# A weight preparation less in the first mixture, and a second layer whose transposes, derivative and projections are one block

## The chip, the cores and the metric

One core of a Trainium2 chip runs the whole network in one launch. Five engines work side by side, each from its own queue in program order, and wait for each other on semaphores: TensorE (PE in the profile; PEld is its weight load), VectorE (DVE), ScalarE (ACT), GpSimd (POOL) and SyncE (SP), which issues the transfers. The metric is the device time of the launch in microseconds, lower is better, as the median of several runs.

## The reference, cut to what matters

The network has two layers over 2048 tokens (2 sequences of 1024) of width 256. The first layer ends in a mixture of 16 experts, of which each token uses four. The second layer begins with a discrete reaction-diffusion derivative of the stream, then differential attention on it:

```python
lap_x = yp_x[:, :, :-2] - 2.0 * y + yp_x[:, :, 2:]      # along the features, reflected
lap_y = yp_y[:, :-2, :] - 2.0 * y + yp_y[:, 2:, :]      # along the tokens, reflected
du_dt = zX * lap_x + zY * lap_y + zR * y * (1.0 - y)
q, k, v = du_dt @ Wq.T, du_dt @ Wk.T, du_dt @ Wv.T      # q is scaled by 32 ** -0.5
```

Then come softmax attention, an output projection, a subject-wise linear layer and a second mixture with one expert for each token.

## The kernel before

**First mixture** (`experts_phase`, L1530 to L1715). TensorE works off jobs of 256 tokens, expert by expert. All engines run loops over pairs of experts in use; the number of pairs is read from a register at run time. While TensorE computes with one expert's weights, SP loads the next and GpSimd splits them into a rounded part and a rest (`split`, casts at L1607 and L1619, subtractions at L1613 and L1623) for single-pass products. `following(p, q)` gives pair `p` the splits 2p+1 and 2p+2, so the last turn loads and splits one set of weights more than TensorE uses. On the last expert `split` of that set runs beside the products. VectorE adds each job's result to the stream `X` at L1709.

**Between the layers** (L2723) all semaphores are cleared behind a barrier of all engines.

**Transposes** (`transpose_phase`, L431): a block of its own. TensorE turns `X` (tokens on partitions) into `hT` (features on partitions) by 32 transposes of 128x128, in 8 groups of 4 with a PSUM bank each; ScalarE and VectorE copy the groups out in turn (L453). A block ends when every engine has ended its part.

**Derivative and projections** (`laplace_phase`, L1718). The tokens are 4 windows of 512 (`w`), the features 2 halves of 128 (`f`); `bank(w, f)` is a PSUM bank for each pair. TensorE first multiplies `hT` by the second-difference operator `lap`, kept among the constants (L1765), 16 full fp32 products of 512 columns. GpSimd sums the two neighbours of each token into `nb` (L1809), then clears `qz`, the zero-padded queries (L1813). VectorE puts the derivative `du` together in four instructions for each (w, f): L1831 and L1832 for the reaction term, L1834 for the neighbours, L1836 for TensorE's part from PSUM. `du` lives in `att`. Then TensorE makes keys (L1750) and queries (L1758), 16 fp32 products each, and values (L1781), 32 of 256 columns. Keys and queries leave PSUM in two parts: ScalarE writes the rounded part (`kh` L1790, `qh` L1795), VectorE the rest (`kl` L1843, `ql` L1850). VectorE copies the values (L1868). GpSimd places the first three tiles of queries into `qz` (`place_queries`, L1879).

A full fp32 product stands in the profile as two MATMUL records. `product3` (L1521) is the cheaper form for operands split in two parts: three single-pass products, high by high, high by low, low by high.

**Attention** (`attention_phase`) is the next block, and needs queries, keys and values.

The diff touches these functions:

## Time and profile before

| what | us |
|---|---|
| median of 3 runs | 1523.15 |
| lowest and highest | 1522.03, 1525.4 |
| the profiled execution, its own time | 1524.83 |
| its span, first to last instruction | 1523.0 |
| last product of the first mixture | 978.0 |
| first transpose of the second layer | 985.4 |
| first instruction of the attention block | 1053.76 |

The profiled execution's time is its span and 1.8 us around it. Its stages are read by their place in the span: the first mixture runs until 978, the change of layers until 985, transposes until 992, derivative and projections until 1053.8, attention after that.

### The profile page before, as it was taken

What the parts mean: (1) busy time and instruction counts of PE and PEld (TensorE: products, weight loads), DVE (VectorE), ACT (ScalarE), POOL (GpSimd) and SP (SyncE); (2) the same over time, 40 slices, a digit from 0 to 9 for tenths busy, and PEclk for the clock granted to TensorE, in tenths of its full rate; (3) what the DMA queues carried; (4) which work ended last, traced back from release to release, by engine and by line L of the source; (5) the groups of instructions that cost most, each with busy time, mean ns of one, the idle gap of its engine ahead of it and who ended that gap; (6) DMA issues with size and microseconds to landing.
All of it is one profiled execution on the core that took longest, in us unless ns stands there. A gap on an engine that the chain in (4) does not pass through costs nothing. (4 is left out here: it accounts for less than half of the span.)

```text
span 1523.0 us, 24894 instructions
## 1 busy us (share of the span) xinstructions
PE 1372.9 (90%) x8678; PEld 1139.8 (75%) x8679; DVE 943.2 (62%) x1708; ACT 722.7 (47%) x1473; POOL 497.7 (33%) x478
## 2 busy tenths in 40 slices
PE   8866799978998789999999999888899899867998
PEld 3345356667895479999999999736688688647997
DVE  4955879965566854454343343395777777464776
ACT  3423877635122246555445556312555456333543
POOL 0331089830000234274062040442211210043885
PEclk9976989989998969999999999999999999988999
DMA  6000000010000014021011000050000000533550
GB/s 235 1 1 0 14 1 1 1 56 1 1 1 0 1 60 162 0 99 67 0 50 60 0 0 0 0 166 1 1 1 1 1 1 1 194 120 115 193 198 20
DMA packets 23244, 69.50 MB, mean 46 GB/s; under 512 B 4419, under 2 KB 8915, under 8 KB 18242
## 3 DMA queue, kind: packets, MB, share of 16 engines
q1 hardware_dynamic: 20866, 62.51, 11.8%
q0 software_dynamic: 2304, 6.03, 1.1%
q8 instruction: 43, 0.70, 0.2%
q14 instruction: 31, 0.25, 0.1%
HBM read 54.62 MB, written 14.19 MB: 45 GB/s over the span
## 5 line engine op out<-in xcount | busy, mean ns | idle before, releaser
L1702 DVE TENSOR_TENSOR ehidl<-hT,ehidh 128x512 fp32r<-128x512 f32 x148 | 140.4, 960 | 136.5 <-ACT ehidh L1685 135.9
L1679 ACT ACTIVATE hT<-ps,eb 128x256 f32<-128x256 f32 x296 | 124.4, 472 | 165.8 <-PE ps L1521 165.8
L2010 ACT ACTIVATE pr<-ps,nmax 128x256 f32<-128x256 f32 (+7 forms) x128 | 94.1, 739 | 103.4 <-DVE nmax L2040 103.3
L1521 PE MATMUL ps<-kh,qz 128*128 128x512 f32 (+3 forms) x384 | 125.3, 380 | 3.3 <-ACT pr L2010 1.9
L1709 DVE SCALAR_TENSOR_TENSOR X<-ps,wE,X 128x256 f32 x74 | 35.8, 484 | 108.3 <-PE ps L1521 98.7
L1685 ACT CAST ehidh<-hT 128x512 fp32r<-128x512 f32 x148 | 91.9, 621 | 4.7
L2040 DVE TENSOR_REDUCE nmax<-ps 128x1 f32<-128x256 f32 (+7 forms) x128 | 91.0, 748 | 1.2 <-PE ps L1950 0.6
L1603 POOL TENSOR_TENSOR eb<-eb1s,consts 128x8 f32<-128x8 f32 x8 | 2.1, 260 | 273.6 <-PE ps L1521 267.3
L1521 PEld LDWEIGHTS ps<-kh,qz 128*128 128x128 f32 x384 | 76.2, 199 | 13.3 <-ACT pr L2010 4.7
L1521 PE MATMUL ps<-ew_1h,ehidh 128*128 128x256 f32 x304 | 85.5, 281 | 0.5 <-POOL ew_1l L1623 0.5
L1521 PE MATMUL ps<-hTh,ew_1h 128*128 x304 | 85.4, 281 | 0.1
L1521 PE MATMUL ps<-ew_1l,ehidh 128*128 128x256 f32 x304 | 85.3, 281 | 0.0
L1521 PE MATMUL ps<-ew_1h,ehidl 128*128 128x256 f32 x304 | 85.3, 281 | 0.0
L1521 PE MATMUL ps<-hTh,ew_1l 128*128 x304 | 85.3, 281 | 0.0
L1521 PE MATMUL ps<-hTh,ew_0h 128*128 x288 | 82.2, 285 | 2.9 <-issue 2.9
L1521 PE MATMUL ps<-hTl,ew_1h 128*128 x304 | 84.7, 279 | 0.0
L1879 POOL CAST qz<-qh 32x256 fp32r<-32x256 f32 x64 | 27.5, 429 | 175.0 <-PE ps L1950 155.3
L1970 PE MATMUL ps<-v,hT 128*128 128x64 f32 x576 | 77.0, 279 | 5.1 <-ACT hT L2001 4.8
L1521 PE MATMUL ps<-hTh,ew_0l 128*128 x288 | 81.6, 283 | 0.0
L1521 PE MATMUL ps<-hTl,ew_0h 128*128 x288 | 81.3, 282 | 0.0
L1521 PE MATMUL ps<-ew_0h,ehidh 128*128 128x256 f32 x288 | 80.5, 280 | 0.0
L1521 PE MATMUL ps<-ew_0l,ehidh 128*128 128x256 f32 x288 | 80.4, 279 | 0.0
(524 smaller groups left out, 4303.1 us busy)
## 6 DMA issues: line engine op xcount, KB each, us to landing
ew1s<-in_ew_dram SPq DMA_DIRECT2D x9, 1024.0 KB, 4.7
ew2s<-in_ew_dram SPq DMA_DIRECT2D x9, 1024.0 KB, 6.8
fw1s<-in_fw_dram SPq DMA_DIRECT2D x8, 1024.0 KB, 7.6
fw2s<-in_fw_dram SPq DMA_DIRECT2D x8, 1024.0 KB, 9.4
slot_rows<-fill SPq DMA_DIRECT2D x1, 5140.0 KB, 20.1
xr<-slot_rows SPq DMA_DIRECT2D x8, 514.0 KB, 4.1
xT<-in_xT_dram SPq DMA_DIRECT2D x4, 512.0 KB, 7.6
X<-in_x_dram SPq DMA_DIRECT2D x1, 2048.0 KB, 18.2
```

The costliest lines, as they stand in the source:

```text
L1521: last = nc.tensor.matmul(out, lhs[a], rhs[b], start=(start and n == 0), stop=(stop and n == 2), **kw)
L1603: nc.gpsimd.tensor_tensor(b1[q][:, :], b1s[q][:, :], k.const("ones", 0, FB), ALU.mult)
L1679: nc.scalar.activation(hid[:, f, :], ps[:, f // 2, (f % 2) * JOB:(f % 2 + 1) * JOB], ACT.Gelu, bias=b1[q][:, f:f + 1]).then_inc(k.e_act, 1)
L1685: nc.scalar.copy(hidp[0][:, f - 1:f + 1, :], hid[:, f - 1:f + 1, :]).then_inc(k.e_dhi, 1)
L1702: nc.vector.tensor_tensor(lo[:, f, :], hid[:, f, :], hi[:, f, :], ALU.subtract).then_inc(k.e_lo, 1)
L1709: nc.vector.scalar_tensor_tensor(x, ps[:, DOWN + t, 0:E], wE2[:, bass.ds(e * NT + blk * TILES + t, 1)], x, ALU.mult, ALU.add).then_inc(k.e ...
L1879: last = nc.gpsimd.tensor_copy(k.qz[r, i % QZ, n, :, s, :], part[r, :, i * P:(i + 1) * P])
L1970: last = nc.tensor.matmul(ps[:, PV + i % 2, h * 64:(h + 1) * 64], dT[:, n % 2, j, :], k.v[:, i - c + j, h * 64:(h + 1) * 64], start=(h == ...
L2010: nc.scalar.activation(pr[:, n % 3, u, 0:wide], half(n, u, wide), ACT.Exp, bias=nmax[:, n % 2, u:u + 1], accum_out=sums[:, u, n:n + 1]).th ...
L2040: nc.vector.tensor_reduce(nmax[:, n % 2, u:u + 1], half(n, u, wide), AX.X, ALU.max, negate=True).then_inc(k.a_max, 1)
```

## The change

In the mixture the pairs of loads and splits are turned by one: load 1 and split 1 come ahead of the loop, and the loop runs one time less (at least once), so the set of weights that no job uses is neither loaded nor split.

In the second layer the transposes lose their block and join `laplace_phase`. The stream, the derivative and the weights are split in two parts and multiplied as single-pass products: two for each step of the second-difference operator (which is rounded only), three for keys, queries and values. ScalarE does all copies of the transposes, the rounded parts, the first half of the reaction term and the copies of the values; VectorE the low parts and the neighbours, which it adds straight from `hT`; GpSimd clears `qz` in six pieces and no longer sums neighbours. The values no longer come last but between the keys and queries of their bank. The order in each queue is written out by hand. The weights are loaded with `wk` first.

```diff
-            return (p * 2 + 1, 1, p + 1) if q == 0 else (p * 2 + 2, 0, p + 2)
+            return p * 2 + (q + 2), q, p + 2
+
+        def later_pairs(eng, name):
+            rest = eng.alloc_register(f"{name}_later_pairs")
+            eng.reg_alu(rest, entry(eng, "pairs", 0, E0 // 2), -1, ALU.add)
+            eng.reg_alu(rest, rest, 1, ALU.max)
+            return eng.snap(rest, min_val=1, max_val=E0 // 2 - 1)
...
-            pairs = entry(sp, "pairs", 0, E0 // 2)
+            rest = later_pairs(sp, "sp")
+
+            def load(s, parity):
+                sp.wait_ge(k.e_s2, s + 1)
+                load_first_mixture(sp, k, entry(sp, "sel", s, E0 - 1), parity)
+
             sp.wait_ge(k.r_b2, NT // 2)
-            with sp.Fori(0, pairs) as p:
+            load(1, 1)
+            with sp.Fori(0, rest) as p:
                 for q in range(2):
                     s, parity, loads = following(p, q)
-
-                    sp.wait_ge(k.e_s2, s + 1)
-                    load_first_mixture(sp, k, entry(sp, "sel", s, E0 - 1), parity)
+                    load(s, parity)
 
         @block.gpsimd
...
-            pairs = entry(pool, "pairs", 0, E0 // 2)
+            rest = later_pairs(pool, "pool")
             for g in range(NT // 2):
                 nc.gpsimd.tensor_tensor(k.X[:, 2 * g:2 * g + 2, 0:E], k.X[:, 2 * g:2 * g + 2, 0:E],
                                         k.bo[g // 4][:, 2 * g % 8:2 * g % 8 + 2, :], ALU.add).then_inc(k.r_b2, 1)
             pool.wait_ge(k.e_s1, 1)
             pool.wait_ge(k.e_s2, 3)
-            with pool.Fori(0, pairs) as p:
+            split(1, 1, 1)
+            with pool.Fori(0, rest) as p:
                 for q in range(2):
...
+            def turn(w, f):
+                for j in range(4):
+                    last = nc.tensor.transpose(ps[:, bank(w, f), j * P:(j + 1) * P],
+                                               k.X[:, 4 * w + j, f * P:(f + 1) * P], k.const("ident"))
+                last.then_inc(k.t_5, 1)
+
+            def second_difference(w, f):
+                pe.wait_ge(k.l_lap, 1)
+                pe.wait_ge(k.l_yl, EB * (w + 1))
+                for j in range(EB):
+                    for n in range(2):
+                        last = nc.tensor.matmul(ps[:, bank(w, f), :], lap[:, j * E + f * P:j * E + (f + 1) * P],
+                                                parts[n][:, j, window(w)], start=(j == 0 and n == 0),
+                                                stop=(j == EB - 1 and n == 1))
+                last.then_inc(k.l_mm, 1)
+
+            def weighted(w, f, weight, done):
+                for j in range(EB):
+                    last = product3(nc, ps[:, bank(w, f), :], [x[:, j, f * P:(f + 1) * P] for x in weight],
+                                    [x[:, j, window(w)] for x in parts], j == 0, j == EB - 1)
+                last.then_inc(done, 1)
+
+            def keys(w, f):
+                pe.wait_ge(k.l_wl, SPLIT.index(KEY) + 1)
+                pe.wait_ge(k.l_dl, EB * (w + 1))
+                weighted(w, f, wk, k.l_km)
+
+            def queries(w, f):
+                pe.wait_ge(k.l_wl, SPLIT.index(QUERY) + 1)
+                pe.wait_ge(k.l_v, EB * w + f + 1)
+                weighted(w, f, wq, k.l_qm)
+
+            def values(w, f):
+                pe.wait_ge(k.l_wl, SPLIT.index(VALUE) + 1)
+                pe.wait_ge(k.l_kl, EB * w + f + 1)
+                for t in range(2):
+                    i = 4 * w + 2 * f + t
                     for j in range(EB):
-                        last = nc.tensor.matmul(ps[:, bank(w, f), :], k.wk[:, j, f * P:(f + 1) * P],
-                                                du[:, j, w * W:(w + 1) * W], start=(j == 0), stop=(j == EB - 1))
-                    last.then_inc(k.l_km, 1)
-
-            def queries(w):
-                for f in range(EB):
-                    pe.wait_ge(k.l_kl, EB * w + f + 1)
-                    for j in range(EB):
-                        last = nc.tensor.matmul(ps[:, bank(w, f), :], k.wq[:, j, f * P:(f + 1) * P],
-                                                du[:, j, w * W:(w + 1) * W], start=(j == 0), stop=(j == EB - 1))
-                    last.then_inc(k.l_qm, 1)
-
-            for w in range(NW):
-                for f in range(EB):
-                    for j in range(EB):
-                        last = nc.tensor.matmul(ps[:, bank(w, f), :],
-                                                k.const("lap", j * E + f * P, P), k.hT[:, j, w * W:(w + 1) * W],
-                                                start=(j == 0), stop=(j == EB - 1))
-                    last.then_inc(k.l_mm, 1)
-            pe.wait_ge(k.s_wC, 64)
-            keys(0)
-            for w in range(1, NW):
-                keys(w)
-                queries(w - 1)
-            queries(NW - 1)
-            for i in range(NT):
-                if i < 8:
-                    pe.wait_ge(k.l_ql, i + 1)
-                else:
-                    pe.wait_ge(k.l_v, i - 7)
-                for j in range(EB):
-                    last = nc.tensor.matmul(ps[:, i % 8, 0:E], du[:, j, i * P:(i + 1) * P], k.wv[:, j, :],
-                                            start=(j == 0), stop=(j == EB - 1))
+                        last = product3(nc, ps[:, bank(w, f), t * E:(t + 1) * E],
+                                        [x[:, j, i * P:(i + 1) * P] for x in parts], [x[:, j, :] for x in wv],
+                                        t == 0 and j == 0, j == EB - 1, skip_group_check=True)
                 last.then_inc(k.l_vm, 1)
+
+            turn(0, 0)
+            turn(0, 1)
+            turn(1, 0)
+            turn(1, 1)
+            second_difference(0, 0)
+            second_difference(0, 1)
+            turn(2, 0)
+            turn(2, 1)
+            second_difference(1, 0)
+            keys(0, 0)
+            keys(0, 1)
+            values(0, 0)
+            turn(3, 0)
+            turn(3, 1)
+            second_difference(1, 1)
+            second_difference(2, 0)
+            values(0, 1)
...
+            def growth(w):
+                b = w // 2
+                act.wait_ge(k.l_z, 1)
+                act.wait_ge(k.l_ya, EB * (w + 1))
+                nc.scalar.activation(du[:, :, window(w)], k.hT[:, :, window(w)], ACT.Identity, bias=z[:, 1, b:b + 1],
+                                     scale=z[:, 0, b:b + 1]).then_inc(k.l_a, 1)
+
+            def high_weight(n):
+                act.wait_ge(k.s_wC, 16 * 4)
+                nc.scalar.copy(PARTS[n][0][:, :, :], WHOLE[n][:, :, :]).then_inc(k.l_wh, 1)
+
+            def operator():
+                nc.scalar.copy(lap[:, :], k.const("lap", 0, EB * E)).then_inc(k.l_lap, 1)
+
+            def high_derivative(w, f):
+                act.wait_ge(k.l_mm, EB * (w + 1))
+                act.wait_ge(k.l_du, EB * w + f + 1)
+                nc.scalar.copy(k.qh[:, f, window(w)], du[:, f, window(w)]).then_inc(k.l_dh, 1)
+
+            def high_keys(w, f):
+                act.wait_ge(k.l_km, EB * w + f + 1)
+                nc.scalar.copy(k.kh[:, f, window(w)], ps[:, bank(w, f), :]).then_inc(k.l_k, 1)
+
+            def values(w, f):
+                act.wait_ge(k.l_vm, EB * w + f + 1)
+                i = 4 * w + 2 * f
+                nc.scalar.copy(k.v[:, i:i + 2, :], ps[:, bank(w, f), :].rearrange("p (t e) -> p t e", t=2)
+                               ).then_inc(k.l_v, 1)
+
+            def high_queries(w, f):
+                act.wait_ge(k.l_qm, EB * (w + 1))
+                nc.scalar.activation(k.qh[:, f, window(w)], ps[:, bank(w, f), :], ACT.Copy,
+                                     scale=SCALE).then_inc(k.l_q, 1)
+
+            high_weight(0)
+            stream(0, 0)
+            high(0, 0)
+            stream(0, 1)
+            growth(0)
+            stream(1, 0)
+            high(0, 1)
+            stream(1, 1)
+            operator()
+            growth(1)
+            high_weight(2)
+            high(1, 0)
+            high(1, 1)
+            high_weight(1)
+            stream(2, 0)
+            high_derivative(0, 0)
+            stream(2, 1)
+            high(2, 0)
...
+            def clear(q):
+                for part in range(2):
+                    nc.gpsimd.memset(k.qz[:, q, part, :, :, :].bitcast(F32), 0.0).then_inc(k.l_zero, 1)
+
+            clear(0)
             nc.gpsimd.memset(k.fill[:, 0:ROWF - 1], 0.0).then_inc(k.z_fill, 1)
             nc.gpsimd.memset(k.fill[:, ID].bitcast(I32), OUTSIDE).then_inc(k.z_fill, 1)
+            pool.wait_ge(k.l_dl, EB * NW)
+            for q in range(1, QZ):
+                clear(q)
             pool.wait_ge(k.z_fill, 2)
-            pool.wait_ge(k.l_zero, 1)
+            pool.wait_ge(k.l_zero, 2 * QZ)
             pool.wait_ge(k.l_ql, EB)
...
+            def neighbours(w):
+                b, first = w // 2, w * W
+
+                def add(at, of, n):
+                    o = du[:, :, first + at:first + at + n]
+                    then(nc.vector.scalar_tensor_tensor(o, k.hT[:, :, first + of:first + of + n], k.row("zy", b), o,
+                                                        ALU.mult, ALU.add))
+
+                dve.wait_ge(k.l_ya, EB * (w + 2 - w % 2))
+                if w % 2 == 0:
+                    add(1, 0, W - 1)
+                    add(0, 1, 1)
+                    add(0, 1, W)
+                else:
+                    add(0, -1, W)
+                    add(0, 1, W - 1)
+                    add(W - 1, W - 2, 1)
+
+            def differences(w, f):
...
+            coefficients()
+            low_weight(0)
+            low(0, 0)
+            growth(0)
+            low(0, 1)
+            neighbours(0)
+            differences(0, 0)
+            differences(0, 1)
+            low(1, 0)
+            growth(1)
+            low(1, 1)
+            low_weight(2)
+            low_derivative(0, 0)
+            low_derivative(0, 1)
+            neighbours(1)
+            low_keys(0, 0)
...
-                transpose_phase(nc, k, k.X, k.hT, None, None, {"mm": k.t_5})
```

The order of all four queues goes on in the same manner to the last window. On TensorE it ends `queries(1, 1)`, `keys(3, 0)`, `keys(3, 1)`, `queries(2, 0)`, `values(2, 1)`, `values(3, 0)`, `queries(2, 1)`, `values(3, 1)`, `queries(3, 0)`, `queries(3, 1)`. On ScalarE `high_queries(0, 1)` stands behind `high_keys(3, 1)`. On VectorE `low_queries(0, 1)` stands right behind `low_derivative(3, 1)`.

## Rows read from the trace of the kernel before

**Rows 1.** The page: busy time of each engine.

```profile
PE 1372.9 (90%) x8678; PEld 1139.8 (75%) x8679; DVE 943.2 (62%) x1708; ACT 722.7 (47%) x1473; POOL 497.7 (33%) x478
```

**Rows 2.** Windows around the change: busy us (instructions) by engine, clock, DMA share.

```profile
978.00:985.30 7.30, 0.00 (x0) 0.00 (x0) 0.64 (x2) 0.00 (x0) 5.50 (x6) 0.78 0.00 0
...
991.70:1008.00 16.30, 13.97 (x32) 6.00 (x32) 15.89 (x11) 0.00 (x0) 13.58 (x9) 1.00 0.26 95
1008.00:1039.00 31.00, 29.74 (x64) 12.59 (x65) 25.72 (x39) 8.87 (x15) 11.18 (x24) 0.94 0.54 154
1039.00:1053.70 14.70, 14.01 (x65) 11.97 (x63) 7.38 (x17) 0.60 (x1) 0.00 (x0) 1.00 0.00 1
```

**Rows 3.** Timeline of GpSimd at the end of the mixture.

```profile
978.66 4.92 POOL L1623 TENSOR_TENSOR ew_0l<-ew2s,ew_0h 128x512 fp32r<-128x512 f32 x4
```

**Rows 4.** Timeline of VectorE, same stretch: the last addition to the stream.

```profile
978.41 0.48 DVE L1709 SCALAR_TENSOR_TENSOR X<-ps,wE,X 128x256 f32 x1 [0.26 <-DVE X L1709]
```

**Rows 5.** Timeline of TensorE: the transposes.

```profile
985.38 5.41 PE L443 MATMUL ps<-consts,X 128*128 128x128 f32 x32 [7.40 <-PEq L2723]
```

**Rows 6.** Windows through the transposes and at attention's start; clock third from last.

```profile
985.30:988.90 3.60, 3.52 (x17) 3.56 (x18) 0.69 (x1) 1.17 (x2) 0.00 (x0) 0.50 0.02 5
988.90:991.00 2.10, 1.89 (x17) 1.65 (x15) 1.56 (x3) 1.17 (x2) 0.00 (x0) 0.99 0.00 0
1053.70:1057.20 3.50, 1.86 (x16) 1.73 (x16) 1.85 (x10) 2.29 (x6) 0.00 (x0) 1.00 0.01 2
1057.20:1060.60 3.40, 2.91 (x16) 2.91 (x17) 1.96 (x10) 1.81 (x10) 0.00 (x0) 0.50 0.00 0
```

**Rows 7.** Timeline of ScalarE: first instruction of the attention block.

```profile
1053.76 1.28 ACT L1994 ACT_TABLE_LOAD   x1 [13.92 <-PEq L1722]
```

**Rows 8.** Groups by line and shape, 960 to 1060 us: busy us, mean ns.

```profile
L1750 PE MATMUL ps<-att,wk 128*128 128x512 f32 x32 | 16.4, 659 | 3.5 <-DVE att L1836 3.4
...
L1831 DVE TENSOR_SCALAR att<-hT,zc 128x512 f32<-128x512 f32 x8 | 11.2, 1397 | 0.0
...
L1834 DVE SCALAR_TENSOR_TENSOR att<-nb,rows,att 128x512 f32<-128x512 f32 x8 | 6.0, 756 | 0.3
...
L1843 DVE TENSOR_TENSOR kl<-ps,kh 128x512 fp32r<-128x512 f32 x8 | 5.3, 684 | 1.4 <-ACT kh L1790 1.3
L1813 POOL MEMSET qz<- 128x6144 f32 x1 | 5.2, 5214 | 0.0
...
L1790 ACT CAST kh<-ps 128x512 fp32r<-128x512 f32 x8 | 4.7, 586 | 30.4 <-PE ps L1750 30.4
```

**Rows 9.** Timeline of TensorE: single-pass products of 256 columns.

```profile
950.24 0.28 PE L1521 MATMUL ps<-ew_0h,ehidl 128*128 128x256 f32 x1
...
950.35 0.28 PE L1521 MATMUL ps<-ew_0h,ehidh 128*128 128x256 f32 x1
```

**Rows 10.** Timeline of TensorE: single-pass products of 512 columns.

```profile
1254.49 0.39 PE L1521 MATMUL ps<-kl,qz 128*128 128x512 f32 x1
1254.71 0.57 PE L1521 MATMUL ps<-kh,qz 128*128 128x512 f32 x2
```

**Rows 11.** Groups by shape on ScalarE, whole span: forms that the change adds.

```profile
L1685 ACT CAST ehidh<-hT 128x512 fp32r<-128x512 f32 x148 | 91.9, 621 | 4.7
...
L244 ACT ACTIVATE modT<-modT,bw 128x1024 f32<-128x1024 f32 x4 | 4.6, 1146 | 3.1 <-DVE modT L334 2.9
```

**Rows 12.** Groups by shape on VectorE, whole span: two inputs, 1024 elements.

```profile
L1250 DVE SCALAR_TENSOR_TENSOR negm<-both_m,fh,negm 128x1024 f32<-128x1024 f32 x1 | 1.3, 1285 | 0.0
```

**Rows 13.** Timeline of SyncE: the issue of the last weight.

```profile
993.11 0.43 SPq L1739 DMA_DIRECT2D wo<-in_wo_dram  x1
```

**Rows 14.** Transfers issued from 985 to 1030 us: KB each, us to landing.

```profile
wo<-in_wo_dram SPq DMA_DIRECT2D x1, 256.0 KB, 4.4
```

**Rows 15.** Timeline of GpSimd: four casts of queries, beside two kinds of VectorE work.

```profile
1022.88 2.59 POOL L1879 CAST qz<-qh 32x256 fp32r<-32x256 f32 x4 [17.50 <-DVE ql L1850]
...
1028.11 1.71 POOL L1879 CAST qz<-qh 32x256 fp32r<-32x256 f32 x4
```

More of the change, by code:

```diff
@@ new lines, in _ @@
+            second_difference(2, 1)
+            keys(1, 0)
+            keys(1, 1)
+            queries(0, 1)
+            second_difference(3, 0)
+            second_difference(3, 1)
+            values(1, 0)
+            keys(2, 0)
+            keys(2, 1)
+            queries(1, 0)
+            values(1, 1)
+            values(2, 0)
+            queries(1, 1)
+            keys(3, 0)
+            keys(3, 1)
+            queries(2, 0)
+            values(2, 1)
+            values(3, 0)
+            queries(2, 1)
@@ L1798, in _, with stream, high @@
-            keys(0)
-            for w in range(1, NW):
-                keys(w)
-                queries(w - 1)
-            queries(NW - 1)
+            def stream(w, f):
+                act.wait_ge(k.t_5, EB * w + f + 1)
+                nc.scalar.copy(k.hT[:, f, window(w)], ps[:, bank(w, f), :]).then_inc(k.l_ya, 1)
+            def high(w, f):
+                act.wait_ge(k.l_ya, EB * w + f + 1)
+                nc.scalar.copy(k.qh[:, f, window(w)], k.hT[:, f, window(w)]).then_inc(k.l_yh, 1)
@@ new lines, in _ @@
+            coefficients()
[14 more added lines that the diff above has]
+            low_keys(0, 0)
+            differences(1, 0)
+            low_weight(1)
+            low(2, 0)
@@ new lines, in _ @@
+            low_keys(0, 1)
+            low(2, 1)
+            growth(2)
+            differences(1, 1)
+            low(3, 0)
+            low(3, 1)
+            low_derivative(1, 0)
+            low_derivative(1, 1)
+            neighbours(2)
+            low_keys(1, 0)
+            differences(2, 0)
+            growth(3)
+            differences(2, 1)
+            low_derivative(2, 0)
+            low_derivative(2, 1)
+            low_keys(1, 1)
+            neighbours(3)
+            differences(3, 0)
```

165 lines of the change are left out of this document (102 added, 63 removed).

## The prediction

> **What bounds the kernel now.** I read the page first: TensorE is busy for 90% of the span [rows 1], so a change counts where TensorE stands idle or where its own work shrinks. Then I cut the change's neighbourhood into windows [rows 2]. From 978.0 to 985.3 TensorE does nothing at all, while GpSimd works for 5.5 us. The timelines say with what: GpSimd's last four subtractions start at 978.66 and end at 983.58 [rows 3], on weights that no job uses, while VectorE's last addition to the stream ends at 978.89 [rows 4]. The transposes start at 985.38 [rows 5], 1.8 us behind GpSimd. So the change of layers waits for GpSimd.
>
> In the second layer the windows show TensorE busy 13.97 of 16.3 us, 29.74 of 31.0 and 14.01 of 14.7, with VectorE beside it at 15.89, 25.72 and 7.38 [rows 2]. First VectorE sets the pace, then both, then TensorE alone with the values. The transposes ran at a granted clock of 0.50 until 988.9 and at 0.99 after it, which are 1.2 and 2.4 GHz [rows 6]. Attention's first instruction is at 1053.76 [rows 7]. From the transposes' block, whose start I put 0.05 us ahead of its first product at 985.33, to there are 68.4 us. That is the stage to be rebuilt.
>
> **Part 1, the mixture.** The last turn's load and split go. The load has been over for long and costs nothing: no transfer runs in 978.0:985.3 [rows 2]. The split ends at 983.58; without it the barrier waits for VectorE at 978.89. I keep the 1.8 us from the last engine's end to the first transpose. Gain: 983.58 - 978.89 = 4.7 us. Bounds: nothing, if something else holds the barrier up; and 5.5 us, GpSimd's whole work in that window. The new order of loads ahead of the loop makes the same loads and splits in the same order, and TensorE's waits there are unchanged: nothing.
>
> **Part 2, work for each engine in the new block.**
> *TensorE.* A full fp32 product of 512 columns takes two records; the window with the second-difference products holds 32 records in 13.97 us, 0.87 us a product, and keys, queries and values are of the same size [rows 2, 8]. So before: 16 + 16 + 16 products and 14.0 us of values, 56 us. A single-pass product of 256 columns starts 0.11 us after the one before [rows 9], one of 512 columns 0.22 us [rows 10]. Now: second difference 32 x 0.22 = 7.1, keys and queries 96 x 0.22 = 21.3, values 96 x 0.11 = 10.6: 39 us. The 32 transposes are the same, 0.11 us each at the full clock (17 records in 1.89 us [rows 6]). TensorE loses 17 us of work, but not 17 us of time, since others now set the pace.
> *ScalarE.* A rounding copy from SBUF of 512 elements costs 0.62 us and one of 1024 with scale and bias 1.15 us [rows 11]; a copy from PSUM 0.59 us [rows 8]. Its queue: 20 copies from SBUF (3 weights, 1 operator, 8 stream, 8 derivative), 4 of 1024, 32 from PSUM: 12.4 + 4.6 + 18.9 = 36 us.
> *VectorE.* From 512 elements 0.68 us without a third operand, 0.76 with one [rows 8]; over 1024 elements with two inputs from SBUF 1.29 us [rows 12]. The neighbours of a window are two such instructions, one on two elements (0.2 us, an estimate: the 0.48 us that L1709 takes for 256 elements [rows 4], less 0.27, half of the step from 512 to 1024 elements) and three waits for the engine's own result: 2.85 us. Its queue: 35 of 0.69, 8 of 0.76, 4 of 1.29, 4 of 2.85: 46.8 us, of which consecutive independent instructions overlap by some 0.08 us each. The 11.2 us of L1831 (1.40 us each, stretched beside GpSimd) and the 6.8 us of value copies are gone, 19 low parts have come.
> *GpSimd.* Clearing qz took 5.21 us [rows 8]; each sixth 0.87. The neighbour sums go.
>
> **Part 3, the four queues laid side by side,** from the block's start T. An instruction starts when its engine is free and its last wait has fallen; from a product's last column to a reader in PSUM I allow 0.2 us, to TensorE from another engine 0.15.
> - ScalarE's queue begins with `high_weight(0)`, which waits for all four weights. The fourth is issued at 993.11, 1.34 us after its block's start [rows 13], and lands 4.4 us later [rows 14]: T + 5.75. Behind it stand all copies of the transposes, so the block as a whole starts there; the four groups of transposes are long done. This is the change's own new wait. Lower bound 4.4, if the issues were no hindrance.
> - ScalarE then needs ten instructions to the end of `operator`: T + 11.4. VectorE's `low(0, 1)` ends at 11.3. TensorE starts the second difference at 11.5, at the low clock after 9.6 us of idling: until 15.1.
> - VectorE: neighbours(0) until 14.1, both differences until 16.0, then low(1, 0), growth(1), low(1, 1), low_weight(2), low_derivative(0, 0) and (0, 1): T + 20.4. Only now may TensorE make keys(0, 0), at 20.5.
> - From neighbours(1) to low_derivative(3, 1) VectorE has 29 steps (3 neighbours, 2 growths, 6 differences, 18 others) of 27.9 us; 2.0 overlap and 0.8 of short waits come in: it ends at T + 47.0. TensorE in that stretch has 25 us of work (10 x 1.33, 5 x 1.32, 5 x 0.89 and two groups of transposes) and short waits.
> - keys(3, 0) follows at 47.4. From there nine products and groups of values stand without a gap: 6 x 1.33 + 3 x 1.32 and two short waits, until 59.6; then ScalarE's two copies and VectorE's last low queries: 61.75.
> - GpSimd may clear four sixths from 47.0, until 50.5, and place queries once low_queries(0, 1) has ended, at 52.1. That is 24 casts in fours of 1.71 us [rows 15], 10.3 us: T + 62.4. It is last, by 0.7 us.
>
> With the full clock throughout, the same working ends at 61.7; with the low clock lasting a few microseconds longer into the keys, at 64.2. I take 63.0 in the middle, and 0.3 us to attention's first instruction (the old block's last value copy ends at 1053.47). So 63.3 against 68.4: gain 5.1 us.
>
> The Trainium skill (TensorE: Matmul & The Clock Gate, Part 4: PE-mode transpose) says that transposes don't bring the full clock. By it the transposes of windows 2 and 3, 16 of them, would cost 0.1 us more each, 1.7 us. The trace speaks against it: through 17 transposes and nothing else the clock was 0.50 and it then rose to 0.99 [rows 6].
>
> **Sum.** 4.7 + 5.1 = 9.8 us off the profiled execution's 1524.83 gives 1515.0; that execution lies 1.7 us above the median of the runs, so the median becomes 1513.3.
>
> **The rivals.**
> *The placing of queries sets the end, at its slow rate.* Four casts took 2.59 us at 1022.88, where VectorE ran two-input additions from SBUF, and 1.71 at 1028.11, where one input came from PSUM [rows 15]. In the new tail VectorE's low keys and queries read one input from PSUM, so I hold it for less likely. At 2.59 the block ends at T + 67.6: 5.2 us more, 1518.5.
> *The clock: slower.* At 1053.70:1057.20 TensorE was busy 1.86 of 3.5 us, and the clock stood at 0.50 for the window after it [rows 6]. If the breaks in the new queue keep it at 0.50 through the keys as well, the last nine products alone cost 12.0 us more, 1525.3; with half of the 25 us in the middle at half speed too, 24.5 us more, 1538. It decides from 9.8 us lost, that is, 9.8 us of TensorE's work at the low clock on the path. Against it: from 20.5 on TensorE has work for over 90% of the time, and the window 1008.00:1039.00 kept 0.94 with a break in it [rows 2].
> *The mixture gives nothing:* the barrier waits for something other than GpSimd. 4.7 us more, 1518.0. GpSimd's end and the transposes' start, 1.8 us apart, speak against it.
> *The start is quicker:* weights at T + 4.4 and the full clock end the block at 60.3, 2.7 us less: 1510.6.
>
> **How the numbers follow.** Forecast 0.60 (own range 1510 to 1517: 61.7 to 64.2 for the clock, and VectorE 5% off either way, 2 us); slow placing 0.12; clock 0.08; nothing from the mixture 0.06; quicker start 0.14. The range takes in the slow placing, the mixture's failure with some of the clock, and below the quick start with 5.5 us from the mixture and VectorE 5% faster: 1507.5 to 1520. A change under 0.2%, 3 us, can't be told from none here. Faster: all but the clock and the chance that two of the dearer cases meet, 0.91. Slower 0.05, the heavy form of the clock; same 0.04, its lighter form or two mishaps.
>
> **What would show it.** The transposes start near 980.7. ScalarE's first instruction of the block is the copy of `wk`, some 5.8 us after that. TensorE idles from about T + 2 to T + 11. VectorE is busy nearly without a break from T + 20 to T + 47. Attention starts near 1044. GpSimd's last cast and VectorE's last low queries end within 1 or 2 us of each other. The prediction is wrong if the weights land later than T + 7, if the clock is below 0.9 from T + 20, if VectorE's instructions over two halves cost well over 1.3 us, or if a wait written by hand stands crosswise so that TensorE idles in its last nine pieces.

## The result, and the profile after

| kernel | median, us | lowest to highest | runs | ratio to before, 95% |
|---|---|---|---|---|
| before | 1522.81 | 1522.03 to 1525.4 | 9 | |
| after | 1516.37 | 1513.87 to 1520.71 | 9 | 0.9957 [0.9947, 0.9968] |

The change makes the kernel faster by 6.4 us; 9.8 were forecast, and 1516.37 against the 1513.3 predicted lies inside the range. The profiled execution after took 1516.37 us, with a span of 1514.6. The page, busy time of each engine [rows 1]:

```profile
PE 1361.2 (90%) x8742; PEld 1147.2 (76%) x8743; DVE 934.0 (62%) x1699; ACT 742.6 (49%) x1509; POOL 470.9 (31%) x459
```

TensorE's busy time is 11.7 us less than before, VectorE's 9.2 and GpSimd's 26.8; ScalarE's is 19.9 more. Windows around the change, with busy us and instructions by engine, clock, DMA share and GB/s [rows 2, 6]:

```profile
976.70:978.40 1.70, 0.00 (x0) 0.01 (x1) 0.00 (x0) 0.00 (x0) 0.03 (x1) 1.00 0.00 0
978.40:984.50 6.10, 1.94 (x16) 1.71 (x16) 1.08 (x2) 0.00 (x0) 2.35 (x4) 0.99 0.79 264
984.50:999.00 14.50, 6.46 (x20) 4.60 (x20) 11.73 (x16) 11.79 (x20) 0.00 (x0) 0.62 1.06 295
999.00:1021.00 22.00, 21.67 (x111) 18.41 (x112) 20.67 (x28) 10.66 (x18) 0.00 (x0) 0.94 0.07 20
1021.00:1040.00 19.00, 19.00 (x111) 16.18 (x109) 9.60 (x16) 8.94 (x17) 10.72 (x23) 1.00 0.00 1
1040.00:1042.90 2.90, 0.09 (x1) 0.00 (x0) 1.29 (x2) 1.09 (x3) 2.36 (x6) 0.92 0.00 0
```

In the first stretch TensorE does nothing; its whole break between the layers is 2.65 us, by the timeline below, where it was 7.40. Then comes a stretch of 6.1 us with 1.94 us of transposes and the transfers at 264 GB/s: the new wait for the weights. From 984.5 VectorE and ScalarE work at 11.7 of 14.5 us each. In 999:1021 VectorE has 20.67 of 22.0, but TensorE has 21.67, and from 1021 TensorE is busy without a break and VectorE half the time. The last 2.9 us are the copies and casts behind the last product.

The timeline of the same stretch, with the last addition to the stream first [rows 3 to 5, 7, 15]:

```profile
976.17 0.48 DVE L1720 SCALAR_TENSOR_TENSOR X<-ps,wE,X 128x256 f32 x1 [0.26 <-DVE X L1720]
```

```profile
978.41 1.94 PE L1766 MATMUL ps<-consts,X 128*128 128x128 f32 x16 [2.65 <-PEq L2936]
990.20 0.76 PE L1775 MATMUL ps<-qh,lapr 128*128 128x512 f32 x1 [9.85 <-ACT lapr L1870]
990.76 0.63 PE L1775 MATMUL ps<-ql,lapr 128*128 128x512 f32 x1
```

```profile
984.50 0.62 ACT L1867 CAST wk_h<-wk 128x512 fp32r<-128x512 f32 x1 [12.86 <-DMA wo<-in_wo_dram]
...
1042.89 1.28 ACT L2207 ACT_TABLE_LOAD   x1 [1.68 <-PEq L1731]
```

```profile
1026.17 3.63 POOL L1953 MEMSET qz<- 128x1024 f32 x4 [45.42 <-DVE ql L2017]
1032.09 1.70 POOL L2092 CAST qz<-qh 32x256 fp32r<-32x256 f32 x4 [2.30 <-DVE ql L2027]
...
1040.88 1.70 POOL L2092 CAST qz<-ql 32x256 fp32r<-32x256 f32 x4
```

The last addition ends at 976.65 and the transposes start at 978.41, 1.8 us behind it. With the block's start T at 978.36, as in the prediction 0.05 ahead of the first transpose, ScalarE begins at T + 6.1, released by the transfer of `wo`; the second difference begins at T + 11.8, and its products stand 0.42 to 0.56 us apart, at the low clock. GpSimd's last casts end at T + 64.2 and attention starts at T + 64.5.

From these rows the way from before to after can be added up by stage, in profiled spans (1523.0 to 1514.6, 8.4 us). Attention is taken from its first instruction to the start of its last product of scores:

| stage | before | after | gain |
|---|---|---|---|
| all ahead of the last addition to the stream, its start | 978.41 | 976.17 | 2.2 |
| from there to T | 6.92 | 2.19 | 4.7 |
| T to attention's first instruction | 68.4 | 64.5 | 3.9 |
| attention, to its last product of scores | 237.6 | 239.3 | -1.7 |
| the rest | | | -0.7 |

The first line can't be put down to the change. In fourteen profiles of kernels with and without it that addition starts between 975.4 and 979.4: at 978.4, 977.5 and 975.4 with the old mixture, at 975.5 to 979.4 with the new. Without it the gain of this pair would be 6.2 us, which is what the medians say. The fourth line was nobody's forecast and needed experiments.

### The profile page after: what moved, and what is told of

Same layout as the page of the kernel before. It is cut to its first block and busy times, and to the rows that moved or that the text cites. A ratio compares the mean times of both kernels' runs of the same rounds, so it can differ in the third digit from the quotient of the medians.

```text
span 1514.6 us, 25020 instructions
## 1 busy us (share of the span) xinstructions
PE 1361.2 (90%) x8742; PEld 1147.2 (76%) x8743; DVE 934.0 (62%) x1699; ACT 742.6 (49%) x1509; POOL 470.9 (31%) x459
## 5 line engine op out<-in xcount | busy, mean ns | idle before, releaser
L1521 PE MATMUL ps<-kh,qz 128*128 128x512 f32 (+3 forms) x384 | 128.5, 388 | 5.5 <-DVE maskb L2237 3.3
L1521 PEld LDWEIGHTS ps<-kh,qz 128*128 128x128 f32 x384 | 78.9, 206 | 15.5 <-ACT pr L2223 4.7
L1521 PE MATMUL ps<-ew_0h,ehidl 128*128 128x256 f32 x288 | 80.6, 280 | 0.0
L2183 PEld LDWEIGHTS ps<-v,hT 128*128 128x128 f32 x576 | 71.4, 196 | 7.5 <-ACT hT L2214 4.7
```

What stands on the lines that cost most here:

```text
L1521: last = nc.tensor.matmul(out, lhs[a], rhs[b], start=(start and n == 0), stop=(stop and n == 2), **kw)
L2183: last = nc.tensor.matmul(ps[:, PV + i % 2, h * 64:(h + 1) * 64], dT[:, n % 2, j, :], k.v[:, i - c + j, h * 64:(h + 1) * 64], start=(h == ...
```

## The experiments

All kernels of an experiment ran beside the kernel before. "Block" is T to attention, "attention" as in the table above, both from the one profiled execution.

| kernel | median, us | ratio to before, 95% | block | attention |
|---|---|---|---|---|
| before | | | 68.4 | 237.6 |
| null_before | 1524.11 | 0.9995 [0.9985, 1.0005] | 69.2 | 237.3 |
| mix_alone | 1519.47 | 0.9957 [0.9944, 0.9970] | 68.2 | 237.4 |
| layer_alone | 1520.95 | 0.9981 [0.9969, 0.9994] | 63.8 | 238.9 |
| after_again | 1516.85 | 0.9950 [0.9933, 0.9966] | 63.9 | 239.0 |
| warm_tail | 1516.84 | 0.9947 [0.9933, 0.9961] | 65.8 | 238.8 |
| warm_head | 1514.46 | 0.9932 [0.9917, 0.9946] | 64.3 | 237.6 |
| start_early | 1512.10 | 0.9910 [0.9893, 0.9927] | 60.5 | 237.6 |
| early_queries | 1514.93 | 0.9937 [0.9922, 0.9953] | 63.7 | 237.6 |
| both_edits | 1512.89 | 0.9932 [0.9919, 0.9945] | 58.9 | 240.4 |
| full_products | 1523.79 | 0.9997 [0.9986, 1.0007] | 70.2 | 237.8 |
| neighbours_pool | 1522.74 | 0.9986 [0.9975, 0.9998] | 69.1 | 239.0 |
| late_attention | 1519.58, one run | | 65.9 | 240.5 |

### The two parts alone

`null_before` is the kernel before under another name, `after_again` the changed kernel, `mix_alone` the change of the mixture with the old second layer, `layer_alone` the reverse: `following(p, q)` and the loops as before, with the new `laplace_phase`.

> The kernel before against itself, profiled a second time. Both theories: a ratio of 1.000 within 0.2%. It is run for its trace. If the change's profile owes its 1.0 us between the mixture's first addition and the second expert, and its 1.8 us more in attention, to chance (the place at which the clock falls), the same stages of this trace lie up to 2 us beside those of the first trace of before. If they are effects of the change, this trace repeats before's within 0.3 us: 68.1 us and 237.6 us.

> The changed kernel once more, for a second trace. Ratio 0.9957 as on record. If attention's 1.8 us more are an effect of the change, its stage again takes 239 us; if chance, it lies anywhere from 237 to 240. The block from first transpose to attention: 64.5 us again by my theory, within 1 us by where the clock rises.

> The mixture's part alone: the unused load and split are gone, the second layer is as before. My theory: the transposes start 1.8 us behind VectorE's last addition and not 6.5 us, 4.7 us less, ratio 0.9969; the block behind it takes its old 68.4 us. Rival, the barrier waits for something else: ratio 1.000. Rival, the turned loop also speeds the mixture's start by the 1.0 us seen in the profile after: 5.7 us less, ratio 0.9963, and the stage from the first addition to the second expert's first product takes 67.1 us and not 68.1.

> The second layer's part alone: the mixture keeps its unused load and split. My theory: the block from first transpose to attention takes 64 to 65 us and not 68.4, attention as before, so 3.9 us less, ratio 0.9974. Rival, attention really takes 1.8 us more behind the new block (its 237.6 us become 239.3, because the clock is worse there): 2.1 us less in all, ratio 0.9986, and attention's stage again near 239.

The same kernel twice comes out at 0.9995, with an interval down to 0.9985. `null_before` also shows how far the block moves by itself: 69.2 us, where the first profile of the same kernel had 68.4. The microsecond between the mixture's first addition and the second expert's first product, of which two expectations speak, is chance: the stage takes 68.0 us in both profiles of before and in `mix_alone`, but 67.0 in `layer_alone`, which has the old mixture, and 67.1 and 67.9 in the two profiles of the changed kernel.

In `mix_alone` the last addition to the stream, on VectorE, and the first transposes, on TensorE:

```profile
979.28 0.48 DVE L1720 SCALAR_TENSOR_TENSOR X<-ps,wE,X 128x256 f32 x1 [0.26 <-DVE X L1720]
```

```profile
981.52 3.84 PE L443 MATMUL ps<-consts,X 128*128 128x128 f32 x21 [2.65 <-PEq L2734]
```

The addition ends at 979.76 and the transposes start at 981.52: 1.8 us again. The stretch from the addition's start to T is 2.2 us, where it was 6.9; the block behind it, 68.2, and attention, 237.4, are those of before. So the mixture is worth 4.7 us, as forecast, in this and in the ten other profiles with it (2.2 us against 6.9 in all of them). The ratio, 0.9957, says 6.6 us with 4.6 at the edge of its interval, which agrees. `layer_alone` has a block of 63.8, 4.6 us shorter, and gives 2.9 us by its ratio: attention takes 1.5 back. By their ratios the two parts add up to 9.5 us, the whole gives 6.5 and 7.6; each interval is 1 to 2 us wide to either side, so these runs do not tell the sum from the whole.

### The wait for the weights

In `start_early` the copy of the first weight no longer stands at the head of ScalarE's and VectorE's queues, but behind `operator` and behind `low(1, 1)`:

```diff
-            high_weight(0)
             stream(0, 0)
...
             operator()
+            high_weight(0)
...
-            low_weight(0)
             low(0, 0)
...
             low(1, 1)
+            low_weight(0)
```

> The changed kernel with the first weight's high part moved behind the operator on ScalarE, and its low part beside the second weight's on VectorE; the stream's copies then don't wait for the weights. My theory: the wait for the weights, 6.1 us from the block's start, sets the block's start, and the block takes 4 to 4.5 us less: 60 us; ratio against before 0.993. Rival, the pace of the keys sets the block and the start only fills a wait: under 1 us less.

The timeline of ScalarE, and of TensorE:

```profile
980.64 0.59 ACT L1852 COPY hT<-ps 128x512 f32<-128x512 f32 x1 [7.43 <-PE ps L1766]
...
985.07 0.63 ACT L1870 CAST lapr<-consts 128x512 fp32r<-128x512 f32 x1
985.59 0.62 ACT L1867 CAST wk_h<-wk 128x512 fp32r<-128x512 f32 x1
```

```profile
979.98 2.81 PE L1766 MATMUL ps<-consts,X 128*128 128x128 f32 x16 [2.64 <-PEq L2936]
985.83 0.76 PE L1775 MATMUL ps<-qh,lapr 128*128 128x512 f32 x1 [3.05 <-ACT lapr L1870]
```

With T at 979.93, ScalarE starts at T + 0.7 on the first transposes and the second difference at T + 5.9, not 11.8. The copy of `wk` comes at 985.59, T + 5.7, about as soon as it did behind its wait, and the first keys wait for VectorE's low part of the derivative, not for it. The block is 60.5 us, 3.5 to 4.1 less than in the two profiles of the changed kernel, and the time 1512.10, with an interval below that of the change. Of the 5.9 us that the start gains some 2 are lost again on the way: the last low part of the derivative ends at T + 43.7 against T + 47.1 and 47.7, and from there the tail is as long as before. The loss goes with the granted clock. A window from T + 14.6 to T + 21.4, clock third from last:

```profile
994.53:1001.36 6.83, 5.97 (x16) 4.84 (x17) 5.76 (x9) 1.07 (x2) 0.00 (x0) 0.50 0.96 284
```

The first keys start at T + 15.5 and run at half the clock for 5.9 us; in the two profiles of the changed kernel they did so for 1.8 and 2.3 us.

### The tail of queries

In `early_queries` ScalarE's `high_queries(0, 1)` moves from behind `high_keys(3, 1)` to right behind `high_queries(0, 0)`. `both_edits` is that and `start_early` together.

```diff
+            high_queries(0, 1)
...
-            high_queries(0, 1)
```

> The changed kernel with the high part of the queries (0, 1) made right behind that of (0, 0) on ScalarE, so that GpSimd can place queries some 2 us sooner. My theory: GpSimd ends last by 0.5 us in the profile after, VectorE's low queries right ahead of it; the block takes 0.3 to 0.6 us less and then ends with VectorE. Rival, the placing alone sets the end: 2 us less.

> The changed kernel with both earlier edits: the first weight's parts behind the operator, and the queries (0, 1) behind (0, 0) on ScalarE. My theory: the gains add, the block takes 59.7 to 60.0 us (60.5 less the 0.5 us by which GpSimd ended behind VectorE); ratio against before 0.990 to 0.991. Rival: with the front shortened another wait sets the end and it stays at 60.5.

The ends of the two queues in `early_queries`, GpSimd's and VectorE's, with T at 980.15:

```profile
1031.45 1.70 POOL L2092 CAST qz<-qh 32x256 fp32r<-32x256 f32 x4
...
1040.23 1.71 POOL L2092 CAST qz<-ql 32x256 fp32r<-32x256 f32 x4
```

```profile
1042.30 1.29 DVE L2027 SCALAR_TENSOR_TENSOR ql<-ps,qh 128x512 fp32r<-128x512 f32 x2 [2.57 <-ACT qh L1889]
```

The casts begin as soon as the clearing of `qz` is over and end at T + 61.8; now VectorE is last, at T + 63.4, and attention starts at T + 63.7 where it started at 63.9 and 64.5. In the changed kernel GpSimd was last by 0.5 us, and half a microsecond is what the edit gives: from the end of TensorE's last product to attention are 2.2 us, where they were 2.8 in both profiles of the changed kernel. In `both_edits` the block is 58.9, better by a microsecond than expected, and 5.0 to 5.6 less than in the changed kernel. That microsecond is the clock's: the first keys start at T + 15.5 again, but the low clock ended 2.9 us sooner than in `start_early`, and the last nine pieces began at T + 43.7, not 44.8.

```profile
994.33:997.75 3.42, 3.02 (x7) 2.47 (x8) 2.96 (x4) 0.09 (x1) 0.00 (x0) 0.50 0.99 290
997.80:1001.00 3.20, 3.12 (x21) 2.59 (x20) 2.65 (x5) 2.18 (x3) 0.00 (x0) 1.00 0.99 278
```

But attention takes 240.4 in its profile, and its ratio, 0.9932, missed the 0.990 to 0.991 expected. Both it and `start_early` are faster than before and than the change: the interval of `start_early` lies below both of the changed kernel's, that of `both_edits` below one of them.

### What each part of the new block carries

`full_products` makes keys, queries and values as full fp32 products from the whole derivative and the whole weights. The parts of the derivative and of the weights are still made, but no product reads them.

```diff
-                    last = product3(nc, ps[:, bank(w, f), :], [x[:, j, f * P:(f + 1) * P] for x in weight],
-                                    [x[:, j, window(w)] for x in parts], j == 0, j == EB - 1)
+                    last = nc.tensor.matmul(ps[:, bank(w, f), :], weight[:, j, f * P:(f + 1) * P],
+                                            du[:, j, window(w)], start=(j == 0), stop=(j == EB - 1))
...
```

> The changed kernel with keys, queries and values as full fp32 products of whole weights and whole derivative; everything else, the low parts too, is still made, only not used there. TensorE's work grows by 0.34 us for each of 16 groups of keys and queries and 0.27 for each of 8 groups of values, 7.6 us. My theory now: from 40 us on TensorE is the pace, and before that VectorE: the block takes 5 to 7 us more than 64 to 64.5, so the single-pass products carry more than the block's whole gain. Rival, VectorE is the pace nearly to the end: at most 3 us more.

Groups by line on TensorE, 978 to 1050 us:

```profile
L1782 PE MATMUL ps<-att,wk 128*128 128x512 f32 x32 | 15.6, 634 | 0.4 <-DVE ql L2017 0.4
L1782 PE MATMUL ps<-att,wq 128*128 128x512 f32 x32 | 14.9, 592 | 0.0
L1802 PE MATMUL ps<-wv,att 128*128 128x256 f32 x64 | 14.9, 380 | 0.0
```

TensorE's busy time in the block, T to attention, in `full_products` and in the changed kernel (first number behind the length):

```profile
978.79:1049.03 70.24, 56.67 (x192) 35.62 (x192) 45.83 (x61) 32.53 (x57) 15.41 (x32) 0.90 0.30 90
```

```profile
978.37:1042.90 64.53, 49.16 (x256) 40.91 (x256) 44.37 (x61) 32.48 (x57) 15.46 (x32) 0.89 0.34 98
```

That is 7.5 us more, as expected. The block is 70.2, 5.7 to 6.3 longer than in the changed kernel and longer than the three of before, 68.2 to 69.2: the cheaper products carry more than the block's whole gain.

`neighbours_pool` lets GpSimd sum the neighbours as before, and VectorE adds the sum in one instruction for each window; GpSimd's first clearing of `qz` moves behind those of `fill`:

```diff
+                nc.gpsimd.tensor_tensor(s[:, :, 1:T - 1], y[:, :, 0:T - 2], y[:, :, 2:T], ALU.add).then_inc(k.l_nb, 1)
...
-                dve.wait_ge(k.l_ya, EB * (w + 2 - w % 2))
-                if w % 2 == 0:
-                    add(1, 0, W - 1)
-                    add(0, 1, 1)
-                    add(0, 1, W)
...
+                dve.wait_ge(k.l_nb, 3 * (b + 1))
+                o = du[:, :, window(w)]
+                then(nc.vector.scalar_tensor_tensor(o, nb[:, :, window(w)], k.row("zy", b), o, ALU.mult, ALU.add))
```

> The changed kernel with the neighbours summed on GpSimd for each sequence, as before, and one addition per window on VectorE: 1.5 us less VectorE work in each of four windows. My theory: VectorE first waits for GpSimd (two sums of 3.6 us and more beside its own additions from SBUF), and TensorE is the pace behind, so nothing is won: block within 1 us of 64.2, or up to 3 us more. Rival, VectorE's load sets the block: 4 to 6 us less.

The timelines of GpSimd and VectorE:

```profile
993.20 3.88 POOL L1963 TENSOR_TENSOR nb<-hT 128x2044 f32<-128x2044 f32 x1 [9.23 <-ACT hT L1853]
997.04 0.34 POOL L1965 TENSOR_TENSOR nb<-hT 128x2 f32<-128x2 f32 x2
1012.62 3.89 POOL L1963 TENSOR_TENSOR nb<-hT 128x2044 f32<-128x2044 f32 x1 [15.24 <-ACT hT L1853]
```

```profile
997.42 1.28 DVE L2005 SCALAR_TENSOR_TENSOR att<-nb,rows,att 128x1024 f32<-128x1024 f32 x1 [3.79 <-POOL nb L1965]
...
1014.10 3.57 DVE L1987 TENSOR_TENSOR ql<-hT,qh 128x512 fp32r<-128x512 f32 x2 [0.25 <-ACT qh L1857]
1017.59 1.28 DVE L2015 TENSOR_TENSOR ql<-att,qh 128x512 fp32r<-128x512 f32 x2
```

It was expected within 1 us of the change to 3 us slower; it is 4.5 to 5.1 us in the block. VectorE waits 3.79 us for the first sum, though its own instruction is then 1.6 us shorter than the three that it replaces. The second sum runs beside VectorE's low parts of the stream: two of them take 3.57 us, 2.96 of it the first, where a pair of the same size takes 1.28 at 1017.59. A third part stands in a window; the clock is third from last:

```profile
1001.20:1007.90 6.70, 5.15 (x12) 3.87 (x13) 4.37 (x6) 1.44 (x3) 0.00 (x0) 0.57 0.39 107
```

TensorE's clock was 0.57 over these 6.7 us, through a second difference and the first keys; in the changed kernel it was back at the full clock 2.3 us into the keys. The clock's part need not be this edit's: `warm_tail`, below, has the same longer stretch at the low clock and a block 1.3 to 1.9 us longer. What is left is by this estimate some 3 us, so taking the sums off GpSimd was most likely a gain of its own.

### The clock at the start

TensorE idles ahead of the second difference, which then runs at the low clock. `warm_head` puts seven full fp32 products of constants into that gap, into a bank not in use:

```diff
+            idle_products(7, 7)
             second_difference(0, 0)
```

> The changed kernel with seven such products behind the first four groups of transposes, in the 10 us in which TensorE waits for the operator. My theory: the second differences then run at the full clock, 0.23 us a product and not 0.43, and the first keys too; the block takes 1.5 to 2 us less than 64.0 to 64.5. Rival, VectorE alone sets the pace there: the products are faster and the block ends no sooner than 64.0.

```profile
993.21 0.47 PE L1775 MATMUL ps<-qh,lapr 128*128 128x512 f32 x1 [2.50 <-ACT lapr L1875]
993.52 0.39 PE L1775 MATMUL ps<-ql,lapr 128*128 128x512 f32 x1
993.75 0.39 PE L1775 MATMUL ps<-qh,lapr 128*128 128x512 f32 x1
```

```profile
983.50:990.00 6.50, 6.50 (x21) 3.52 (x20) 1.39 (x2) 2.37 (x5) 0.21 (x2) 0.94 1.01 339
...
1001.50:1004.40 2.90, 2.71 (x7) 2.16 (x8) 2.75 (x4) 0.00 (x0) 0.00 (x0) 0.50 0.43 124
```

The clock is at 0.94 over the window with the added products, and the second difference starts with products 0.23 us apart. Its eighth ends at T + 14.5, 0.7 to 1.1 us sooner. But the keys run at 0.50 all the same, and low_derivative(0, 1) ends at T + 20.2 as in the changed kernel (20.2 and 20.6): VectorE sets the pace there. The block gains nothing, 64.3. The rival held.

### Attention's 1.5 us

Attention is unchanged and takes 237.3 to 237.8 us in seven profiles, 238.8 to 240.5 in the other seven. A window in the changed kernel, 167 us into attention, and the same place in the kernel before; clock third from last:

```profile
1209.80:1213.20 3.40, 3.40 (x15) 2.99 (x14) 1.96 (x4) 1.36 (x4) 0.37 (x1) 0.52 0.00 0
```

```profile
1220.30:1223.60 3.30, 3.30 (x26) 3.04 (x26) 2.60 (x5) 1.77 (x6) 0.44 (x2) 1.00 0.00 0
```

TensorE is busy throughout in both, with 15 products at a clock of 0.52 in the one and 26 at 1.00 in the other: 11 products less, at 0.13 us each 1.4 us. Each of the seven longer profiles has this stretch at the low clock, 3.4 us long; it begins 165.7 to 167.9 us behind attention's start, and none of the shorter seven has it. Just ahead of it TensorE has three short breaks, of 0.12, 0.27 and 0.76 us, and the clock falls within 0.5 us of the third one's end; but the shorter seven have the same three breaks, and it does not fall there. Two of the seven, `both_edits` and `late_attention`, have a further one at 45 us and take 240.4 and 240.5.

The first theory was that TensorE's idling ahead of attention brings it. `warm_tail` fills that gap with three full fp32 products behind the last queries, with results that nothing uses.

```diff
             queries(3, 1)
+            pe.wait_ge(k.l_ql, 1)
+            idle_products(3, 0)
```

> The changed kernel with three full fp32 products (512 columns, of constants, result unused) behind the last queries, into a bank already read; some 2.6 us in which TensorE otherwise waits for the block's end. My theory: attention's 239.0 to 239.3 us in the three traces with the new block, against 237.4 to 237.6 in the three with the old one, come from TensorE idling some 3 us ahead of attention, so that the clock is low for 10 to 14 us at its start. Then the stage returns to 237.5 us and the low stretch to 7 us, 1.6 us less in all, ratio against before 0.994. Rival, attention is slower for another reason (layout, queues): the stage stays at 239 us.

The theory fell. Attention's first 5.3 us were at the full clock (3.4 in the kernel before, none in the changed one), but the stretch is there, and attention took 238.8:

```profile
1209.80:1213.20 3.40, 3.40 (x16) 2.93 (x14) 1.96 (x4) 1.29 (x4) 0.40 (x1) 0.59 0.00 0
```

Nor does the low clock at attention's start cost anything that shows: in `early_queries` it lasts for attention's first 10 us, and attention takes 237.6. The block of `warm_tail` is longer, 65.8, because its first keys ran at half the clock for 5.9 us and not for 2.3: the low clock lasted 6.8 us there, as in `neighbours_pool` and `start_early`.

The second was that the clock's steps stand at fixed places and attention's start moves among them. `late_attention` delays attention with five such products in place of three.

> The changed kernel with five unused full products behind the last queries: the block ends 0.5 to 1.5 us later than in warm_tail's order of 64.2. All four traces with attention at 238.7 us or more have a stretch of low clock some 166.5 us behind attention's first instruction, none of the six at 237.4 to 237.6 has one. My theory: it is where the clock's steps fall relative to attention, and no effect of the change: the moved start gives 237.5 and no such stretch, more likely than not. Rival: the new block brings it in any case: 239 again.

It took 240.5, where 237.5 was held for more likely. The fourteen traces still speak for this theory. Each has another stretch at the low clock, which begins 128.8 to 131.6 us behind attention's start and so shows where the clock's steps stood. Sorted by it, the profiles with and without the later stretch fall into groups:

| that stretch begins, us behind attention's start | the later stretch |
|---|---|
| 128.8, 128.9, 129.0, 129.2 | in all four |
| 129.3, 129.5, 129.7, 129.7 | in none |
| 130.2, 130.4 | in both, and the one at 45 us |
| 130.8, 130.9 | in neither |
| 131.6, 131.6 | in one of two |

This order was found afterwards, and no experiment placed the steps on purpose. So the stretch, and its price, are shown; what decides that it comes is not. It is no property of the new block: `start_early`, `early_queries`, `warm_head` and `full_products` have new blocks and attention at 237.6 to 237.8.

## Why the prediction was right, and where it was short

- **The mixture: right.** 4.7 us forecast, 4.7 measured in eleven profiles with it against three without, with the 1.8 us of the barrier kept.
- **The wait for the weights: right.** T + 5.75 forecast, 5.1 to 6.5 in the nine profiles with the wait; `start_early` shows that it is a wait on the path, and worth 3.5 to 4.1 us. It is the largest thing that the change left lying.
- **VectorE sets the pace to T + 47: right to T + 20.** In the three profiles of the unedited block (the two of the changed kernel and `layer_alone`) low_derivative(0, 1) ended at T + 20.2 to 20.6 (20.4 forecast), and low_derivative(3, 1) at T + 47.0 to 47.7 (47.0). Its three instructions over two halves cost what was forecast, 2.85 us. But keys(3, 0), which the forecast started right behind the second, started 1.1 us after it: TensorE came to them late. `growth` was forecast at 1.15 us on ScalarE and takes 1.25, and on TensorE's side 0.22 and 0.11 us for a product were 0.23 and 0.12:

```profile
1024.38 0.28 PE L1521 MATMUL ps<-wv_h,qh 128*128 128x256 f32 x1
1024.50 0.29 PE L1521 MATMUL ps<-wv_l,qh 128*128 128x256 f32 x1
...
1027.20 0.39 PE L1521 MATMUL ps<-qh,wk_h 128*128 128x512 f32 x1
1027.43 0.39 PE L1521 MATMUL ps<-ql,wk_h 128*128 128x512 f32 x1
```

```profile
L1996 DVE SCALAR_TENSOR_TENSOR att<-hT,rows,att 128x1024 f32<-128x1024 f32 x4 | 5.1, 1281 | 0.1
...
L1862 ACT ACTIVATE att<-hT,zc 128x1024 f32<-128x1024 f32 x4 | 5.0, 1245 | 0.1
```

- **The mis-sized term is TensorE's work from T + 20 on.** The prediction gave it 25 us of work in the 26.9 from the first keys at T + 20.5 to keys(3, 0) at T + 47.4, and 12.2 for the last nine pieces. In the profile after, the first keys start at T + 20.8 and keys(3, 0) at T + 48.8, and in these 28.0 us TensorE's longest break is 0.18. By the measured distances the 25 are some 26.5, and the first keys at half the clock for 2.3 us add some 1.2:

```profile
999.10:1001.60 2.50, 2.44 (x6) 1.99 (x7) 2.43 (x3) 0.00 (x0) 0.00 (x0) 0.53 0.56 155
1001.70:1004.00 2.30, 2.12 (x12) 1.55 (x11) 1.52 (x4) 1.32 (x3) 0.00 (x0) 1.00 0.00 0
```

  The last nine pieces therefore began at T + 48.8, not 47.4: 0.3 us for the later first keys and 1.1 for TensorE's own work. In the prediction's sum TensorE had slack in the middle; in these profiles it has none, and 4% on each product is on the path. It was so in `after_again` and `layer_alone` too, where the same stretch takes 27.8 and 27.6 us.
- **The casts of the queries: right in kind.** They were forecast last by 0.7 us and are by 0.5; they took 1.71 us for four, never the 2.59 of the slow rival. They begin at T + 53.7, 1.6 us later than forecast, 1.4 of it for the later nine pieces, and stand 1.75 apart, so that six groups take 10.5 us and not 10.3.
- **So the block:** 62.7 forecast for the low clock at the start, plus 1.4 for the later nine pieces and 0.4 for the casts, is 64.5, as measured. The middle value 63.3 left 0.6 for the clock. The unedited new block takes 64.5, 63.9 and 63.8 in its three profiles, the old one 68.4, 69.2 and 68.2 in its three: by their means the gain is 4.5 us where 5.1 were forecast, and by single pairs 3.7 to 5.4.
- **The cheaper products:** not a step in the sum by themselves, but `full_products` shows that without them the new order would be slower than the old.
- **The clock:** the rival that lost most did not come; the clock was 0.94 in 999:1021 and 1.00 behind it. In the profile after, the transposes ran at 0.99 from the first, behind a break of 2.65 us and not 7.40. That is no rule: behind the same break `warm_tail`, `warm_head` and `neighbours_pool` began them at the low clock.
- **Not foreseen: attention.** The forecast left it as it was. In this profile it took 1.7 us more, in `after_again` 1.4. With 4.7 and 4.5 that leaves 7.5 to 7.8 of the 9.8; the medians say 6.4 and the interval 4.9 to 8.1. Whether the change makes the extra stretch likelier isn't known: it stood in neither profile of before, nor in `mix_alone`, and in three of three with the new block unedited.

The likeliest case was the right one, near the upper end of its own range of 1510 to 1517. Of the 3.4 us that the medians are short of the forecast, some 0.6 are in the block and 1.4 to 1.7 in attention; the rest is less than these runs can tell. The time came out inside the range although attention's part was in no rival: it is the width of the range, not a term of the sum, that held it.

## What to carry to other kernels

When a change moves the bound from one engine to another, sum the second engine's whole queue as closely as the first's: here the sum left TensorE 1.9 us of slack in 26.9, and 4% more for each product and 2.3 us at half the clock used it up. In a queue written by hand, look at the head for an instruction that waits for a transfer while ready work stands behind it: moving the first weight's copy and its low part gave 3.5 to 4.1 us, nearly as much as the whole rebuilt block. And measure a stage beside its own start and end, since a gain of 4 us in a block can lose 1.5 in an unchanged stage behind it.

## What the runs showed of the hardware

- A stretch of 3.4 us at half clock in unchanged work, with TensorE busy throughout it, costs about 1.4 us (15 products where there were 26). It stood in seven of fourteen profiles, and in those the clock fell behind three breaks of TensorE of 0.76 us at the most, which the other seven have too; what decides stays open.
- Seven full fp32 products in an idle gap left the first six products behind them at the full clock (0.23 us apart, not 0.43), and it was low again for the keys, behind a break of 2.3 us: products added for the clock's sake gained nothing in the block.
- The change of layers, from the last engine's end to the first transpose, took 1.8 us in every profile, whether GpSimd or VectorE was last.
- Two of VectorE's subtractions with both inputs in SBUF took 3.57 us beside GpSimd's sum, and 1.28 without it. The first of them took 2.96 and ended 0.55 us behind that sum, about its own time. By the Trainium skill (SBUF — State Buffer, Who interferes with whom) a VectorE operation with two SBUF inputs and a GpSimd operation that reads SBUF exclude each other for a whole instruction; the trace agrees.
- Four weights of 256 KB, issued at the start of a block beside a transfer of 5140 KB, had all landed 5.1 to 6.5 us behind its start, in nine profiles.
